# An attention and expert kernel: all engines step by pairs of heads, and TensorE's products are regrouped

## What is computed

```python
xn = layernorm(x)
# attention: 16 heads of 64; rotary on the first 32 of each head's dimensions of Q and K
scores = where(causal, -inf, Q @ K.T) / sqrt(64)
attn_out = softmax(scores) @ V            # heads side by side, then @ W_o.T
# experts: 8 of them, 128 -> 512 -> 128, top 2 of 9 choices; the ninth is "keep xn"
gates = top_2(softmax(xn @ router_w + router_b))
ffn_out = sum_e gates[e] * (gelu(xn @ w1[e]) @ w2[e]) + gates[8] * xn
out = x + attn_out + ffn_out
```

## Time and profile before

| | |
|---|---|
| median of 3 runs (lowest to highest) | 1568.7 us (1566.03 to 1572.05) |
| the profiled execution: its time / its span | 1575.69 us / 1574.0 us |
| PE busy | 1302.8 us, 83% |
| PE weight loads | 1005.9 us, 64% |
| DVE / ACT / POOL busy | 1155.5 / 1130.1 / 849.2 us (73, 72, 54%) |
| mean granted TensorE clock | 0.952 of 2.4 GHz |

### The profile page before, as it was taken

The page is one execution under the profiler, slowest core; times in us unless marked ns, Lnnn a source line. Parts: engine busy times, 40 slices in busy tenths (PEclk is TensorE's granted clock), DMA queues, the critical chain, the costliest instruction groups (busy, mean ns, idle before and its releaser), DMA issues.

```text
span 1574.0 us, 46446 instructions
## 1 busy us (share of the span) xinstructions
PE 1302.8 (83%) x15156; PEld 1005.9 (64%) x15157; DVE 1155.5 (73%) x4018; ACT 1130.1 (72%) x3606; POOL 849.2 (54%) x1194
## 2 busy tenths in 40 slices
PE   2416999999898999877999997888888888888878
PEld 1304676677676666656898895666666666666656
DVE  5787777776777777655777777777777778778776
ACT  6415787788877887775788887677777777777766
POOL 3244777777777777661000004666666666666655
PEclk9657999999999999997999999999999999999999
DMA  9621433333333333341232322333333333333330
GB/s 287 188 50 38 89 75 71 69 70 79 88 71 69 79 88 70 69 122 46 84 87 83 87 85 53 81 73 75 75 86 77 74 79 76 79 81 77 75 75 25
DMA packets 115831, 130.12 MB, mean 83 GB/s; under 512 B 11568, under 2 KB 75312, under 8 KB 115376
## 3 DMA queue, kind: packets, MB, share of 16 engines
q1 hardware_dynamic: 107056, 110.26, 29.5%
q0 software_dynamic: 8576, 17.33, 3.9%
HBM read 28.85 MB, written 31.59 MB: 38 GB/s over the span
## 4 chain that ended last, share of the span: by engine, by line
DMA 25%; PE 22%; POOL 18%; DVE 17%; issue 13%; ACT 4%; SPq 0%; POOLq 0%; DVEq 0%; ACTq 0%
DMA sorted_x_dram<-stage,slots 16%; DMA stage<-sorted_y_dram,slots 7%; PE bank L1087 5%; PE bank L1088 5%; PE bank L1089 5%; POOL arena L454 4%; DVE arena L947 4%; POOL arena L453 3%; POOL sorted_x_dram L493 3%; POOL arena L478 2%; DVE arena L910 2%; ACT probs L640 2%; POOL stage L484 2%; PE bank L1158 2%; DVE arena L909 1%
## 5 line engine op out<-in xcount | busy, mean ns | idle before, releaser
L640 ACT ACTIVATE probs<-arena,neg_max 128x128 f32<-128x128 f32 (+1 forms) x1024 | 455.5, 449 | 235.1 <-DVE neg_max L947 223.2
L947 DVE CUSTOM_DVE_ANT_0 arena<-bank,causal 128x128 f32<-128x128 f32 (+1 forms) x1024 | 302.8, 350 | 25.4 <-PE bank L1158 23.6
L1168 PE MATMUL bank<-ident,probs 128*128 128x128 f32 x1536 | 248.9, 277 | 69.3 <-DVE probsT L969 56.5
L503 POOL DMA_INDIRECT stage<-sorted_y_dram,slots x128 | 126.9, 991 | 260.4 <-DMA sorted_y_dram<-stage 238.0
L1168 PEld LDWEIGHTS bank<-ident,probs 128*128 128x128 f32 x1536 | 183.1, 143 | 107.7 <-ACT probs L640 70.2
L1195 PE MATMUL bank<-probsT,arena 128*64 128x256 f32 x1024 | 226.6, 415 | 19.0 <-ACT probsT L623 18.4
L1158 PE MATMUL bank<-arena 64*128 64x128 f16 (+1 forms) x3072 | 175.0, 248 | 28.0 <-DVE neg_max L947 25.8
L640 ACT ACTIVATION_READ_ACCUMULATOR probs<-arena,neg_max 128x1 f32 x1024 | 197.4, 193 | 0.0
L493 POOL DMA_INDIRECT sorted_x_dram<-stage,slots x128 | 131.1, 1024 | 115.1 <-DMA sorted_x_dram<-stage,slots 92.7
L623 ACT ACTIVATE probsT<-bank 128x384 f32<-128x384 f32 x384 | 186.1, 485 | 7.0 <-PE bank L1168 6.5
L473 POOL TENSOR_TENSOR arena<-o_whole,arena 128x256 f16<-128x256 f32 x256 | 173.0, 676 | 21.2
(11 more groups left out here) (152 smaller groups left out, 3297.9 us busy)
## 6 DMA issues: line engine op xcount, KB each, us to landing
arena<-arena SPq DMA_DIRECT2D x256, 256.0 KB
arena<-sorted_x_dram SPq DMA_DIRECT2D x72, 128.0 KB, 2.2
sorted_y_dram<-stage SPq DMA_DIRECT2D x72, 128.0 KB, 1.8
sorted_x_dram<-arena SPq DMA_DIRECT2D x3, 2304.0 KB, 17.8
arena<-experts_dram SPq DMA_DIRECT2D x8, 512.0 KB, 5.4
out_dram<-acc SPq DMA_DIRECT2D x32, 128.0 KB
sorted_x_dram<-arena SPq DMA_DIRECT2D x1, 2368.0 KB, 18.7
sorted_x_dram<-stage,slots POOLq DMA_INDIRECT x128, 2.3
```

Source lines behind the costliest of these rows:

```text
L640: last = nc.scalar.activation(probs[:, s % 4, at:at + w], masked[:, s % 4, at:at + w], ACT.Exp, bias=neg_max[:, s % 4, t:t + 1], scale=-1. ...
L947: last = nc.vector.tensor_tensor_reduce(out=masked[:, (s + i) % 4, at:at + w], in0=SC[i][:, at:at + w], in1=causal[:, at:at + w], scale=1. ...
L1168: last = nc.tensor.transpose(TP[s % 2][:, k * P:(k + 1) * P], probs[:, s % 4, k * P:(k + 1) * P], ident[:])
```

## The change

The unit of the order becomes the pair of heads, a period p of 0 to 7 for every engine, and all lags count periods (T_LAG 1, PV_LAG and OUT_LAG 2, INV_LAG 3, SPLIT_LAG 4, BACK_LAG 2). In a period PE runs scores of p, turn_sums of p-3, the units (fp16), and then the transposes of both heads of p-1 and attend of p-2 (fp32). Sums are turned one period after their attend. Evictions of p-2 stand first in ACT's and DVE's period. The units are packed anew: two a period in most, one in periods 3 and 4. Which heads DVE evicts goes from 0, 4, 8, 12 to 2, 4, 6, 8. Each period has one send or one gather, a gathered row is combined two periods later, and `normalise_row` waits for the sends of its stage buffer's last use, where it waited for all sends before it. The numbers of products, copies and DMAs stay as they are.

```diff
+PAIRS = H // 2
+OPENERS = ((0, "rope", 0), (0, "rest", 0), (1, "rope", 1), (1, "rest", 1), (2, "v_high", 0), (2, "rest", 2),
+           (3, "rope", 2), (3, "v_high", 1), (4, "rope", 3), (4, "rest", 3))
+USUAL = ((0, "rope", 1), (0, "rest", 2), (1, "rope", 2), (1, "rest", 3), (2, "rope", 3), (2, "v_high", 0),
+         (3, "v_high", 1), (4, "y", 0), (5, "y", 1))
+AHEAD = ((5, "rest", 0), (6, "rope", 0), (7, "rest", 1))
+VALUES = ((6, "v_low", 0), (7, "v_low", 1))
-T_LAG, OUT_LAG, PV_LAG, O_LAG, SCALE_LAG, SPLIT_LAG = 3, 4, 5, 6, 7, 8
+T_LAG, PV_LAG, OUT_LAG, INV_LAG, SPLIT_LAG, BACK_LAG = 1, 2, 2, 3, 4, 2
+DVE_TURNED = (2, 4, 6, 8)
...
+        def past(b, p, lag):
+
+            return (b, p - lag) if p >= lag else None if b in (0, MID) else (b - 1, p - lag + PAIRS)
...
@@ POOL @@
-                pool.wait_ge(sent, 16 * TOP * tile)
+                if tile >= PER:
+                    pool.wait_ge(sent, 16 * TOP * (tile - PER + 1))
...
+                for p in range(PAIRS):
+                    then = past(b, p, SPLIT_LAG)
+                    if then:
+                        o_split(8 * then[0] + then[1], then[1], then[0] % 2)
+                    for kind, j, of, u, psum in due(b, p, 2):
+                        if kind == "rope" and j < 2:
+                            q_rope_low(j, of)
+                    if b < MID:
+                        if p % TOP == 0:
+                            normalise_row(b, p // TOP)
+                        send(b, p)
+                    else:
+                        gather(b, p)
+                    for kind, j, of, u, psum in units_at(b, p):
                         if kind == "rope":
                             rope_add(j, of)
...
@@ ACT @@
+                for p in range(PAIRS):
+                    turned(past(b, p, OUT_LAG))
+                    then = past(b, p, INV_LAG)
+                    if then:
+                        o_copy(8 * then[0] + then[1], then[1])
+                    for s in (2 * p, 2 * p + 1):
+                        exps(b, s, at == OPENING)
+                    for kind, j, of, u, psum in units_at(b, p):
                         if kind == "rest":
                             rest_high(j, u, psum, of, True)
                         elif kind in ("v_low", "v_high"):
                             v_copy(kind, j, u, psum, 16 * of - 8 if kind == "v_low" else None if at == OPENING else 16 * of)
+                    for kind, j, of, u, psum in due(b, p, 1):
                         if kind == "rope":
                             rope_high(j, of)
...
@@ DVE @@
+                for p in range(PAIRS):
+                    turned(past(b, p, OUT_LAG))
+                    for kind, j, of, u, psum in due(b, p, 1):
+                        if kind == "rest":
+                            rest_low(j, psum, of)
+                    masks(b, 2 * p)
+                    for kind, j, of, u, psum in units_at(b, p):
+                        if kind == "rope":
+                            turn(j, u, psum, of)
+                    then = past(b, p, INV_LAG)
+                    if then:
+                        o_scale(8 * then[0] + then[1], then[1])
+                    then = past(b, p, 2)
+                    if then and p % 2 == 0:
+                        invert(4 * then[0] + then[1] // 2, then[1] // 2)
+                    for kind, j, of, u, psum in due(b, p, 2):
+                        if kind == "rope" and j >= 2:
+                            rope_low(j, of)
+                    if p == 0:
+                        if b >= MID:
+                            mix(b)
+                        elif b > 0:
+                            mix(b - 1)
+                    then = past(b, p, BACK_LAG)
+                    if then and b >= MID:
+                        combine(*then)
+                    for kind, j, of, u, psum in units_at(b, p):
+                        if kind == "y":
+                            y_add(of, j, u, psum, at in (FORMER, TURN))
...
@@ PE @@
+            def transposes(b, p, at_first):
+
+                for s in (2 * p, 2 * p + 1):
+                    pe.wait_ge(exp_done, 16 * b + s + 1)
+                    if not (at_first and p == 0):
+                        pe.wait_ge(*(evicted(b, s - 2) if p else evicted(b - 1, s - 2 + H)))
...
+                for p in range(PAIRS):
+                    scores(b, 2 * p, parity, at == OPENING)
+                    then = past(b, p, INV_LAG)
+                    if then:
+                        turn_sums(*then)
+                    for kind, j, of, u, psum in units_at(b, p):
+                        unit(kind, j, of, of % 2, psum, bank_free(u))
+                    then = past(b, p, T_LAG)
+                    if then:
+                        transposes(*then, then[0] == 0)
+                    then = past(b, p, PV_LAG)
+                    if then:
+                        attend(*then, at)
```

More of the change, by code:

```diff
@@ L89 @@
     if _b in (MID - 1, B - 1):
-        UNITS += [(_b, H, "y", t, _b) for t in range(TPS)]
+        UNITS += [(_b, PAIRS, "y", t, _b) for t in range(TPS)]
 def attention_and_experts(nc, x, wqk, wvo, rw, rb, experts, tables, sorted_x, sorted_y, out):
@@ L255, in evicted @@
         def evicted(b, s):
-            return (t_out[0], 4 * b + s // 4 + 1) if s % 4 == 0 else (t_out[1], 12 * b + s - s // 4)
+            before = sum(1 for turned in DVE_TURNED if turned <= s)
+            return (t_out[0], 4 * b + before) if s in DVE_TURNED else (t_out[1], 12 * b + s + 1 - before)
+        def past(b, p, lag):
+            return (b, p - lag) if p >= lag else None if b in (0, MID) else (b - 1, p - lag + PAIRS)
         def former_samples(body):
@@ L273, in latter_samples, with units_at, due @@
             body(B - 1, 1, FINAL)
-        def units_at(b, s):
-            return [(kind, j, of, u, PJ[u % PJ_BANKS]) for u, (at, step, kind, j, of) in enumerate(UNITS) if (at, step) == (b, s)]
-        def due(b, s, lag):
-            return units_at(b, s - lag) if s >= lag else [] if b in (0, MID) else units_at(b - 1, s - lag + H)
+        def units_at(b, p):
+            return [(kind, j, of, u, PJ[u % PJ_BANKS]) for u, (at, period, kind, j, of) in enumerate(UNITS) if (at, period) == (b, p)]
+        def due(b, p, lag):
+            then = past(b, p, lag)
+            return units_at(*then) if then else []
         def parts(kind, j):
@@ L647, in sample @@
                     act.wait_ge(early_low, EARLY)
-                for s in range(H):
-                    for kind, j, of, u, psum in due(b, s, 1):
+                for p in range(PAIRS):
[6 more added lines that the diff above has]
+                    for kind, j, of, u, psum in units_at(b, p):
                         if kind == "rest":
@@ L1018, in sample, with turned @@
-            def sample(b, parity, at):
-                for s in range(0, H, 2):
-                    masks(b, s)
-                    beside(b, s, at)
-                    beside(b, s + 1, at)
+            def turned(then):
+                if then:
+                    for s in (2 * then[1], 2 * then[1] + 1):
+                        if s in DVE_TURNED:
+                            t_evict(16 * then[0] + s, s % 4)
+            def sample(b, parity, at):
+                for p in range(PAIRS):
[27 more added lines that the diff above has]
+                            y_add(of, j, u, psum, at in (FORMER, TURN))
@@ L1024, in rest_of @@
             def rest_of(b, at):
-                t_evict(16 * b + 12, 0)
-                o_scale(8 * b + 4, 4)
+                o_scale(8 * b + 5, 5)
                 invert(4 * b + 3, 3)
-                o_scale(8 * b + 5, 5)
                 o_scale(8 * b + 6, 6)
@@ L1031, in rest_of @@
                     mix(b)
+                else:
+                    for k in range(PAIRS - BACK_LAG, PAIRS):
+                        combine(b, k)
                 o_scale(8 * b + 7, 7)
-                for kind, j, of, u, psum in units_at(b, H):
+                for kind, j, of, u, psum in units_at(b, PAIRS):
                     y_add(b, j, u, psum, at == TURN)
@@ L1160, in scores @@
                 last.then_inc(s_ready, 1)
-            def transposes(G, s, free):
-                pe.wait_ge(exp_done, G + 1)
-                if free is not None:
-                    pe.wait_ge(*free)
-                for k in range(3):
-                    last = nc.tensor.transpose(TP[s % 2][:, k * P:(k + 1) * P], probs[:, s % 4, k * P:(k + 1) * P], ident[:])
-                last.then_inc(t_ready, 1)
+            def transposes(b, p, at_first):
[3 more added lines that the diff above has]
+                        pe.wait_ge(*(evicted(b, s - 2) if p else evicted(b - 1, s - 2 + H)))
+                    for k in range(3):
+                        last = nc.tensor.transpose(TP[s % 2][:, k * P:(k + 1) * P], probs[:, s % 4, k * P:(k + 1) * P], ident[:])
+                    last.then_inc(t_ready, 1)
             def turn_sums(b, j):
```

108 lines of the change are left out of this document (22 added, 86 removed).

## The result

The changed kernel takes 1506.5 us (median of 4 runs, 1500.74 to 1508.37), 0.9595 of the time before (95% interval 0.9564 to 0.9627): 62 us faster where 145 were forecast, and 14 us above the range.

What follows compares the result with a forecast made beforehand. TensorE was taken as the bound: its 29.6 us floor plus 0.7 for shapes plus waits gave samples of 31.7 (former) and 33.4 (latter). Savings of 58, 75 and 12 sum to 145 us: forecast 1424 us, range 1375 to 1492.

Steps and rivals of the forecast that it cites:

- What bounds the kernel: TensorE is nearest its limit: 29.6 us a sample without waits, measured samples 6.2 and 9.1 above, which the change can win.
- The shape cost: PE's array changes shape four times a pair, not three: 0.09 each, 0.7 us a sample (0 to 1.4).
- Wait (a): A pair's second head, evicted late, has its attend run serially on PE: 0.60 us a pair; was to go.
- Wait (b): PE's "y" unit waits 1.25 us for POOL's last split of the sample before; was to shrink to 0 to 0.3.
- Wait (c): Latter half: DVE's combine waits 1.48 us for its gathered row, which goes, then takes 2.07, which stays.
- The density: Units packed two a period in periods 0 to 2 make PE wait: 1.4 us a former sample, 3.1 a latter.
- B: Rival: DVE and ACT take PE's place as the bound; 77 us saved, 1492 us; chance 0.27.
- C: Rival: PE held at transposes that wait for an evicted bank; 76 us slower, 1644 us; chance 0.05.
- D: Rival: waits only move, shape cost and dense periods eat all of (a) to (c); 1565 us; chance 0.04.
- The edges: Samples 0, 15, 16 and 31 keep their own waits for DMA and weights; 3 us gained each, 12 in all.

Runs made afterwards that it cites:

- invert_first: The changed kernel with the inversion of the row sums moved from near the end of DVE's even periods to their start: 1470.3 us, ratio 0.9397.
- before_combines_later: The kernel before with five of its eight combines one head later, nothing else: 1534.1 us, ratio 0.9766.
- sends_moved: Changed kernel, inversion first; former half: Q remainders and normalised rows on DVE, sends 2 to 4 a period earlier; latter half: mix in period 3; 1440.0 us.

## Why the prediction was right or wrong

**What bounds the kernel.** This is the step that failed. "TensorE is the engine nearest its limit" is true, and the limit of the former half was another: a chain of waits on POOL, which was busy 26.1 of 35.85 us and looked idle a quarter of the time. The prediction goes by busy shares and PE's waits, takes the wait for POOL's split as one wait of 1.25 to be moved away, and puts a send into POOL's sum at 1.04 and its landing at nothing. The question not asked was what POOL itself waits for. In the kernel before that is 84.0 us for landings; they are worth 4.3 us a sample there (35.85 to 31.55) and 4.1 in invert_first.

**The shape cost** was nearly right. A period with two units is 3.81 to 3.82 us, forecast 3.79, and 3.70 in the order with one change of shape less. Six transposes until attend take 0.75, of which 0.66 are their own; attend until scores takes 0.81 where attend until sums took 0.70. Scores until sums is 0.60, as scores until attend was 0.59; both change the shape, so that row tells no price. The rule "Mode switching requires drain" (Trainium skill, "TensorEngine Tiling (Array Packing)", Key Properties) fits the 0.09 to 0.12 at the other passages where the shape changes. What a sample takes with no wait at all is by these periods 6 x 3.82 + 3.16 + 4.51 = 30.6, forecast 30.3.

**Wait (a)** was right in kind: all attends run side by side. The count was near too: 51 late pairs in 14 samples, about four in each where I took five, by 0.9 us in the median. What it had wrong is that these 3.0 us a sample could be won by themselves. With the sends left out of the kernel before, one late pair a sample is left, of 0.90; the others were late because of the landings, and while these set the pace, moving the evictions won 0.5 in all (35.85 to 35.33).

**Wait (b)**, priced at 0 to 0.3, still was 1.0 in the former half, in 13 samples of 14:

```profile
279.21 0.22 PE L1102 MATMUL bank<-wvo_lo,arena 128*128 128x128 f16 x1 [1.02 <-POOL arena L476]
```

I had counted POOL's instructions (14.4 us against 11.4) and it was to come 3 us late into period 3; it waits for the landings too, and its send of period 7 starts 6.9 us behind PE's start of that period. A send that I costed at 1.04 keeps the next one back for 2.3 to 5.1 us from its start (the medians above), as far as no other work fills the time.

**Wait (c)**: the DMA wait went, as forecast. The 2.07 went too, which I had said would stay: the longest is 0.88. before_combines_later shows the same with the old order. The price of each combine, 0.56, was right for the kernel before and nearly so after: the mean of the 104 is 0.56 and then 0.50.

**The density** allowance of 3.1 for the latter half was right in its releaser (DVE) and mostly in its place (3.0 us a sample of PE's waits in periods 1 and 3, but 1.0 in period 7), and too low for one order of DVE's work: with the inversion first the latter sample is 32.63, better than the forecast's 33.4; as the change was made it is 35.31. I had listed the inversion and the mix behind DVE's 10.2 of 11.4 us, and had not followed that PE's very first product after the scores waits for that inversion. For the former half the allowance of 1.4 (bounds 0 and 1.9) should have been 5.0 (35.33 less 30.3), landings included. The bound of 1.9 was not a bound: it took the waits of the kernel before for all that there could be, and left out that they hide one another.

**The TensorE clock** was not in the sum. Before, the latter half had 0.97, after 1.00. In the windows of the kernel before, 4 us in which PE was busy 1.54 and then 4 us at 0.58, so mostly at the lower of its two levels (1.2 GHz):

```profile
1040.00:1044.00 4.00, 1.54 (x11) 0.87 (x9) 3.94 (x12) 1.49 (x6) 1.85 (x3) 1.00 0.29 42
1044.00:1048.00 4.00, 4.00 (x37) 2.78 (x36) 3.34 (x14) 2.86 (x11) 2.96 (x5) 0.58 0.91 214
```

In windows of one sample each, one is granted 0.91, seven 0.96 and five 1.00, 0.37 of a window of 39 us in all: up to 14 us of the latter half's 45 are the clock. The clock's records in the trace have nine stretches of 3.4 us at the lower level there. Each begins at a wait of PE of 2.1 to 2.5 us, between 0.4 before its end and 1.4 after it. But not each such wait has one: of 17 waits of 2.0 us or more eight have none, and between 1080 and 1084 PE was busy 1.53 and the clock stayed at 1.00. before_combines_later has two such stretches in its latter half, so a part of its gain is the clock as well.

**The rivals.** B's 1492 is nearest to the time, for a reason that doesn't hold: DVE and ACT keep all their work in invert_first, which takes 1470. C (PE held at transposes) didn't happen: those waits are 2.4 us in the whole latter stretch, and DVE ended them. D (nothing gained) was nearly true of the former half, but by a limit that neither it nor any other case named; with the sends left out it is true there as D tells it, 31.55 us a sample before and 31.57 in the new order with the inversion first.

**The edges**, 12 us forecast, were 19: 4.6, 9.1 and 8.9, less the 3.5 of sample 30.

**Open.** Why a send lands in 4 to 5 us beside the stacking DMAs is not shown by a run that takes the stacking away. Two things are under way there, SP's DMAs and DVE's busiest periods. The DMA packets in the trace of the kernel after speak for the transfers. Of the 112 sends of samples 1 to 14, 69 have at most five packets of other queues starting before they land: their first packet starts 1.6 us after the send, and they land in 2.32 (median). For 42 there are 109 to 443 such packets; their first starts 2.9 after the send, and they land in 4.42 (medians). But a few land late without company: in period 7 two sends with the same instructions beside them on DVE and POOL, to within 0.05 us, landed in 2.31 and in 3.82. Also open are the 2.0 us a sample that sends_moved has above the kernels without landings; beside the 54.8 us for landings, POOL waits 33.1 us before sends there until DVE's turn has ended.

## What to carry to other kernels

Before calling the busiest engine the bound, read the waits of each engine that feeds it, its waits on its own DMAs too: an engine at 73% whose instructions are chained to landings can be the one that sets the pace, and moving the others' work then gains next to nothing. A wait that is seen in many places, like the late evictions here, can be the far end of one chain; leaving that chain out in a run shows how many of them are its own. When an order is rewritten with longer distances, list for the first instruction of each engine's period what it waits for and where that stands in the other engine's period; a small step at the end of one and at the head of the next costs more than a large one in the middle. To tell work from waiting, put an instruction of about the same length in the place of the DMA.

## What the runs showed of the hardware

An indirect DMA from POOL of 128 rows landed 2.3 us after its start when little else moved (median; 3.8 at most), and 3.3 to 5.1 (medians of periods 2 to 4, 5.6 at most) while the eight stacking DMAs of SP were under way. The view of the tile, former stretch of the kernel after, has it all in one line:

```profile
DMA to landing us min/median/max: 2.3/2.6/5.6
```

A DVE instruction on 128x8 elements, which takes 0.17 us at its shortest, took 1.17 beside a POOL instruction of 1.15, and half of them took 0.35 or more (durations in ns, min/median/max):

```profile
L970 DVE TENSOR_SCALAR inv_parts<-inv_total x116: 171/350/1174, 161.1 to 1422.4; 128x8 f16<-128x8 f32 x116
```

Of all 128 in the trace, the 21 with no POOL instruction beside them took 0.171 to 0.173 us each; the 29 beside POOL's rope sum alone (L456, L457) took 0.35 to 0.36.

The exclusive lock that the Trainium skill describes ("SBUF — State Buffer", section "SBUF: two separate sides") fits the 1.17, which ends with POOL's instruction. But it is told there of instructions in a two-port mode or with two SBUF inputs; this one has a single small input, and no run here shows in which mode it is.
